# Attention with a routed low-rank layer on one core: how the first head pair and the last weight halves are prepared

## The reference

```
xn = layernorm(x)
q, k, v = xn @ Wq + bq, xn @ Wk + bk, xn @ Wv + bv      # 16 heads of 64
att = softmax(causal(q k^T / 8)) / 8
z = att v, laid out as (s, h * dh) without a transpose of h and s; out1 = z @ proj
base = xn @ W^T
p = l2norm(xn @ Wp^T + bp);  s = l2norm(sim) * exp(min(temp, CLAMP_MAX))
lw = softmax(p @ s);  ret = lw where it is the largest, else 0     # 4 experts
res = sum over the experts of ret * (xn @ Wd_i^T) @ Wu_i^T         # ranks 1, 2, 4, 8
return x + out1 + base + res
```

## Time and profile before

| | us |
|---|---|
| median of 3 runs | 1351.15 |
| lowest and highest of them | 1350.88 and 1351.46 |
| the profiled execution | 1350.67 |
| its span in the trace | 1348.9 |
| of the span: TensorE busy | 1330.2 (99%) |
| VectorE busy | 1106.4 (82%) |
| ScalarE busy | 1086.5 (81%) |
| GpSimd busy | 998.3 (74%) |

### The profile page before, as it was taken

How to read it: one execution, slowest core, us unless ns; L and a number is a source line. 1 busy time by engine, 2 the same in 40 slices (tenths; PEclk the granted TensorE clock), 3 DMA queues, 4 the chain that set the end, 5 groups by cost and what they waited for, 6 DMA issues and landing times.

```text
span 1348.9 us, 34446 instructions
## 1 busy us (share of the span) xinstructions
PE 1330.2 (99%) x10783; PEld 1131.2 (84%) x10783; DVE 1106.4 (82%) x4000; ACT 1086.5 (81%) x3161; POOL 998.3 (74%) x1441
## 2 busy tenths in 40 slices
PE   6999999999999999999999999999999999999998
PEld 4788888888888888888888888888888888888887
DVE  7988888788887878878788787888878888787884
ACT  5887888888878887887888788788888887888785
POOL 6887876778777786777777768777677876778764
PEclk9999999999999999999999999999999999999999
DMA  5444444544545445444544544454454454445441
GB/s 154 103 107 117 114 111 105 128 107 103 124 108 123 98 115 126 103 117 108 120 104 115 124 101 114 113 121 110 104 119 116 103 122 115 118 99 120 112 103 48
DMA packets 112706, 150.85 MB, mean 112 GB/s; under 512 B 18256, under 2 KB 47247, under 8 KB 112527
## 3 DMA queue, kind: packets, MB, share of 16 engines
q1 hardware_dynamic: 111662, 148.36, 46.4%
q10 hardware_dynamic: 864, 0.29, 0.1%
HBM read 10.69 MB, written 4.19 MB: 11 GB/s over the span
## 4 chain that ended last, share of the span: by engine, by line
PE 95%; ACT 1%; DVE 0%; issue 0%
PE zp L1311 22%; PE ptp L1287 20%; PE jobp L1157 13%; PE scores L1275 9%; PE scores L1278 7%; PE outp L1323 7%; PE jobp L1162 6%; PE scores L1256 4%; PE scores L1253 3%; PE jobp L1172 1%; PE outp L1332 1%; ACT prob L720 1%; PE jobp L1177 1%; PE jobp L1348 0%; PE jobp L1167 0%; PE outp L1337 0%
## 5 line engine op out<-in xcount | busy, mean ns | idle before, releaser
L631 POOL TENSOR_TENSOR prob<-prob,rden 128x128 f32<-128x128 f32 (+3 forms) x1024 | 713.9, 722 | 250.7 <-DVE rden L960 244.8
L971 DVE CUSTOM_DVE_ANT_0 prob<-scores,mask 128x128 f32<-128x128 f32 (+3 forms) x1024 | 471.3, 487 | 201.5 <-issue 131.9
L720 ACT ACTIVATE prob<-prob,nmax 128x128 f32<-128x128 f32 (+3 forms) x1024 | 567.5, 559 | 14.7 <-DVE nmax L971 7.8
L1287 PE MATMUL ptp<-ident,prob 128*128 128x128 f32 x2560 | 367.1, 274 | 1.9 <-ACT pt L731 1.5
L1287 PEld LDWEIGHTS ptp<-ident,prob 128*128 128x128 f32 x2560 | 295.0, 140 | 27.7 <-POOL prob L631 4.1
L1311 PE MATMUL zp<-pt,v_sb 128*64 128x64 f32 (+3 forms) x4096 | 307.7, 303 | 0.8 <-DVE z_lo L989 0.8
L731 ACT ACTIVATE pt<-ptp 128x128 f32<-128x128 f32 (+3 forms) x512 | 221.4, 432 | 102.8 <-PE ptp L1287 102.8
L1311 PEld LDWEIGHTS zp<-pt,v_sb 128*64 128x64 f32 x4096 | 221.6, 137 | 51.9 <-issue 20.3
L983 DVE COPY pt<-ptp 128x128 f32<-128x128 f32 (+3 forms) x512 | 243.0, 475 | 3.8 <-PE ptp L1287 2.9
L574 POOL CAST k_low<-k_lo 64x512 fp32r<-64x512 f32 x256 | 156.3, 611 | 77.0 <-DVE k_lo L860 67.0
L1275 PE MATMUL scores<-k_twice,q_parts 128*128 128x384 f32 (+1 forms) x512 | 201.3, 393 | 0.8 <-DVE nmax L971 0.8
(11 more groups left out here) (188 smaller groups left out, 2002.2 us busy)
## 6 DMA issues: line engine op xcount, KB each, us to landing
k_twice<-k_hi SPq DMA_DIRECT2D x508, 128.0 KB, 2.3
q_parts<-q_lo SPq DMA_DIRECT2D x256, 128.0 KB, 2.5
q_parts<-q_hi SPq DMA_DIRECT2D x254, 128.0 KB, 2.3
xin<-in_L_attn_x_dram SPq DMA_DIRECT2D x16, 256.0 KB, 4.2
xres<-in_L_attn_x_dram SPq DMA_DIRECT2D x16, 256.0 KB, 3.1
out_dram<-osb SPq DMA_DIRECT2D x15, 256.0 KB, 2.6
pt<-in_L_attn_Wq_dram SPq DMA_DIRECT2D x1, 512.0 KB, 5.2
pt<-in_L_attn_Wk_dram SPq DMA_DIRECT2D x1, 512.0 KB, 6.1
```

What stands on the lines that cost most here:

```text
L631: nc.gpsimd.tensor_tensor(part, part, scale, ALU.mult).then_inc(pn_ready, 1)
L720: nc.scalar.activation(part, part, ACT.Exp, bias=nmax[:, s % NROT, h:h + 1], scale=-1.0, accum_out=den[:, s % NROT, h:h + 1]).then_inc(p_r ...
L971: nc.vector.tensor_tensor_reduce(out=prob[:, s % NROT, h, 0:cols], in0=scores[bank][:, first_col:first_col + cols], in1=mask[:, S - cols:S ...
L1287: done = nc.tensor.transpose(ptp[h][:, P * j:P * j + P], prob[:, s % NROT, h, P * j:P * j + P], ident[:])
```

## The change

- **Crossing halves.** VectorE makes `swap`, the identity with its column halves exchanged. TensorE multiplies the q low part and `k_hi` of pair 0 by it into `scores[0]` and `outp`. ScalarE copies the results into the other halves of `q_parts` and `k_twice` (four copies of 64 rows by 512). The two DMAs on SP and the two on ScalarE's queue go, and the loads of `proj` no longer wait for them. For pair 1 of the first batch GpSimd copies the two k high parts that stay in their half, and SP issues two DMAs where it issued four. The load of the next batch's `xin` follows the k moves of step 0 and no longer precedes them.
- **The gate's setup.** `sim` and `temp` are loaded by ScalarE's queue at the very start. VectorE's square, sum and clamp, GpSimd's root and ScalarE's exponential move into the gaps of the prologue. `similar_units` runs before the first maximum.
- **The later low halves.** For parts 3, 4, 5 ScalarE makes a second copy of the bank, unrounded, into unused columns of `v_sb` (`raw_weights`). GpSimd subtracts it (`low_weights`, a 128x512 subtraction) at steps 8, 9 and 10, in the order 5, 3, 4. TensorE's jobs of steps 10, 11 and 12 wait for the first, second and third of them. ScalarE does all of parts 3 and 4 after the exponentials of step 0, and evacuates q and k of pair 1 before these.
- **Places in the first batch.** `projection_parts` moves from steps 6 and 10 to 11 and 14, the sum from 14 to 17, `experts_up` from 13 to 18, and the statistics from 5 and 9 to 9 and 17.

```diff
+STEP_SPLIT, STEP_SUMMED, STEP_UP, STEP_BIAS_BANK, STEP_BIAS = (11, 14), 17, 18, 20, 22
+STEP_REST = {8: 5, 9: 3, 10: 4}
+FIRST_STATS = (9, 17)
...
+        w_raw = {k: v_sb[:, k - 2, S:2 * S] for k in (3, 4, 5)}
+        swap = wut
...
+            def low_weights(k):
+                n, half, _ = parts[k]
+                cols = slice(S * half, S * half + S)
+                pool.wait_ge(w_raw_ready, k - 2)
+                nc.gpsimd.tensor_tensor(w_lo[n][:, cols], w_raw[k], w_hi[n][:, cols].bitcast(F32), ALU.subtract)\
+                    .then_inc(w_rest_ready, 1)
...
                     if s in JOBS and JOBS[s][0] == "k" and not (last and s in AHEAD):
                         pad_low_keys(c, s)
+                    if b == 0 and s in STEP_REST:
+                        low_weights(STEP_REST[s])
...
+            def raw_weights(k):
+                nc.scalar.activation(w_raw[k], parts[k][2][:], ACT.Copy).then_inc(w_raw_ready, 1)
...
             job(setup, FIRST_K)
-            act.wait_ge(job_hi[bank_of(FIRST_K)], setup.hi(FIRST_K))
+            act.wait_ge(q_swapped, 1)
             for h in range(2):
-                act.dma_start(k_twice[other(h), h, 0, :].bitcast(F32),
-                              k_hi[own(h), :].bitcast(F32)).then_inc(qk_moved[0], 16)
+                nc.scalar.activation(q_parts[other(h), h, 0, :], scores[0][other(h), :], ACT.Copy).then_inc(crossed, 1)
             weights(2)
-            weights(3)
-            weights(4)
+            act.wait_ge(k_swapped, 1)
+            for h in range(2):
+                nc.scalar.activation(k_twice[other(h), h, 0, :], outp[other(h), :], ACT.Copy).then_inc(crossed, 1)
...
+            pe.wait_ge(swap_ready, 2)
+            pe.wait_ge(job_done[bank_of(FIRST_Q)], setup.job(FIRST_Q))
+            nc.tensor.matmul(scores[0][:], swap[:], q_lo[:, 0, :], start=True, stop=True).then_inc(q_swapped, 1)
+            pe.wait_ge(job_hi[bank_of(FIRST_K)], setup.hi(FIRST_K))
+            nc.tensor.matmul(outp[:], swap[:], k_hi[:], start=True, stop=True).then_inc(k_swapped, 1)
...
+                if first and s in (NBLK * 2 + 2, NBLK * 2 + 3, NBLK * 3):
+                    pe.wait_ge(w_rest_ready, s - NBLK * 2 - 1)
                 if not tail and s in JOBS and not (last and s in AHEAD):
                     job(c, s)
```

More of the change, by code:

```diff
@@ L432, in rows, with move @@
                 return t[bass.ds(b, 1), :, :].rearrange("o (n p) e -> p (o n) e", p=P)
-            def move(c, s):
+            def move(c, s, halves=(own, other)):
                 kind, n = JOBS[s]
@@ L444, in move @@
                     else:
-                        for half in (own(h), other(h)):
-                            sp.dma_start(k_twice[half, h, n % 2, :].bitcast(F32),
+                        for half in halves:
+                            sp.dma_start(k_twice[half(h), h, n % 2, :].bitcast(F32),
                                          k_hi[own(h), :].bitcast(F32)).then_inc(moved, 16)
@@ L457, in batch @@
                 first, last = b == 0 if isinstance(b, int) else False, b is last_batch
-                if not last:
-                    sp.wait_ge(xn_ready, c.at(1, 1))
-                    sp.dma_start(xin[:], rows(x, b + 1)).then_inc(xin_loaded, 16)
                 for s in MOVED_STEPS:
                     if s < STEP_FINAL:
-                        move(c, s)
+                        move(c, s, (other,) if first and s == 0 else (own, other))
+                    if s == 0 and not last:
+                        sp.wait_ge(xn_ready, c.at(1, 1))
+                        sp.dma_start(xin[:], rows(x, b + 1)).then_inc(xin_loaded, 16)
                 if not first:
@@ L480, in _ @@
             sp.wait_ge(job_done[bank_of(FIRST_Q)], setup.job(FIRST_Q))
-            for h in range(2):
-                sp.dma_start(q_parts[other(h), h, 0, :].bitcast(F32),
-                             q_lo[own(h), 0, :].bitcast(F32)).then_inc(qk_moved[0], 16)
-            sp.wait_ge(qk_moved[0], setup.moved(NPAIR))
             for half in range(2):
@@ L599, in _ @@
             pool.wait_ge(heads_marked, 4)
+            pool.wait_ge(job_hi[bank_of(0)], Counts(pool, 0).hi(0))
+            for h in range(2):
+                nc.gpsimd.tensor_copy(k_twice[own(h), h, 1, :], k_hi[own(h), :].bitcast(F32)).then_inc(own_copied, 1)
+            pool.wait_ge(own_copied, 6)
             def projection_parts(half):
@@ L734, in _ @@
             setup = Counts(act, -1)
+            act.dma_start(sim_b[:].rearrange("p a b -> p (a b)"),
+                          sim.rearrange("a b -> (a b)").partition_broadcast(P)).then_inc(sim_loaded, 16)
+            act.dma_start(temp_b[:], temp.partition_broadcast(P)).then_inc(sim_loaded, 16)
             act.wait_ge(zeroed, 3)
@@ L769, in step @@
                 if not tail:
-                    if s - 1 in evacuated(s) and s - 1 in JOBS and not (last and s - 1 in AHEAD):
+                    if s - 1 in evacuated(s) and s - 1 in JOBS and not (last and s - 1 in AHEAD) and not (first and s == 1):
                         job(c, s - 1)
@@ L773, in step @@
                         job(c, UNITS - 1, back=1)
+                    if s == 0 and first:
+                        job(setup, LATER[2])
+                        job(c, 0)
                     if s == STEP_EXPERTS:
@@ L791, in batch @@
                     if first and s == 0:
-                        job(setup, LATER[2])
-                        gate_factor()
+                        for k in (3, 4):
+                            weights(k)
+                            raw_weights(k)
                     if first and s == 1:
                         weights(5)
+                        raw_weights(5)
             batch(0, True, False)
@@ L885, in _ @@
             variances(before)
+            dve.wait_ge(consts_ready, 1)
+            for half in range(2):
+                nc.vector.tensor_copy(swap[:, own(half)], ident[:, other(half)]).then_inc(swap_ready, 1)
             dve.wait_ge(rstd_ready, 1)
@@ L946, in similar_units @@
                 nc.vector.tensor_scalar(simn[:], sim_unit[:], gate_scale[:, 0:1], None, ALU.mult).then_inc(simn_ready, 1)
+            similar_units()
             def value_bias():
@@ L1091, in step @@
                         job(c, js)
-                if s in STEPS_STATS and not last:
-                    statistics(c, STEPS_STATS.index(s))
+                for half, due_step in enumerate(FIRST_STATS if first else STEPS_STATS):
+                    if s == due_step and not last:
+                        statistics(c, half)
                 if s == STEP_AGGR and not last:
@@ L1103, in batch @@
                     if first and s == 0:
-                        weights(3)
                         job(before, LATER[2])
-                    if first and s == 1:
-                        weights(4)
-                        weights(5)
-                    if first and s == 2:
-                        similar_units()
                     if first and s == STEP_UP:
@@ L1262, in score @@
                 if i == 0:
+                    if first and p < 2:
+                        pe.wait_ge(own_copied, 4 + 2 * p)
                     if first and p == 0:
-                        pe.wait_ge(own_copied, 4)
-                    pe.wait_ge(qk_moved[p % 2], c.moved(p))
+                        pe.wait_ge(crossed, 4)
+                    wait(pe, qk_moved[p % 2], c.moved(p))
                     pe.wait_ge(low_padded, c.values(p, 1))
@@ L1295, in values @@
                     wait(pe, z_ready, c.pair(p - 1))
+                    if c.b == 0 and p == 0:
+                        pe.wait_ge(w_raw_ready, 3)
                 if h == 0 and p in (0, NPAIR // 2):
```

50 lines of the change are left out of this document (25 added, 25 removed).

## The result

The changed kernel takes 1356.43 us in the median of six runs (1355.5 to 1357.83), the kernel before 1351.21 beside it. The ratio is 1.0039, with an interval of 1.003 to 1.0049: **5.2 us slower**, and above the range of the forecast (1350.8 to 1356.0). The profiled execution took 1357.83 us (span 1356.1), 7.16 more than the one of before. It is the longest of the six, and one of the two whose mean granted clock was 0.999 and not 1.0. So the two traces differ by 2 us more than the medians, and a reading that sets one trace against the other has to say which part is of the change.

A forecast was written before the change was run, and what follows sets the result against it. TensorE was taken to bound the kernel from about 48 us, so the first batch decides. Terms +0.2 - 0.9 + 4.05 - 0.5 = +2.85 us on a median of 1351.15 gave 1354.0 us, range 1350.8 to 1356.0.

The forecast's parts named there:

- The place: The case is decided in the first batch, before TensorE becomes the bound at about 48 us.
- the chain behind E: GpSimd's pad(3), n(9), n(10) and three subtractions hold TensorE's jobs of steps 10 to 12: +4.05 us.
- E: The end of VectorE's k low part of pair 3 in the first batch, 43.17 us in the kernel before.
- the first loads: Prologue: sim and temp loaded ahead of Wq's end on a second queue cost +0.2 us, ends 0 and +0.4.
- the sum: Whole kernel: +0.2 - 0.9 + 4.05 - 0.5 = +2.85 us on the median.
- The crossing: Prologue: v jobs 0.5 us later, cancelled by ScalarE's earlier q of pair 1; otherwise up to 0.5 lost or 0.3 gained.
- ScalarE at steps 0 to 3: From 19.03 to 28.87 us, 3.2 us of added work into 2.7 of slack makes q of pair 2 +0.3 later.
- E 0.9 earlier: First batch: VectorE's k low part of pair 3 ends 0.9 us earlier, through moved statistics and a shorter router's group.
- The router group: VectorE at step 9, first batch: 1.98 us before, 0.7 us shorter because GpSimd idles then.
- the chain is late as well: Rival, chance 0.20: late k moves of pair 2, dearer first loads and an unshortened router's group give +4.15 us, 1355.3.
- Recovery: After TensorE's job of step 12, two of its waits for ScalarE and VectorE vanish: -0.5 us, ends 0 and 0.9.
- The milepost: Start of TensorE's job of step 12 (k of pair 4), 47.10 us before, forecast near 50; the rest follows at fixed distance.

The follow-up runs named there:

- e2_gate_back: Changed kernel with the gate's loads and setup put back where the kernel before has them: 1355.02 us against 1351.44, ratio 1.0029.
- e5_early_temp: Kernel before with only temp (0.5 KB) loaded by ScalarE's queue at the start, sim staying on SP: 1352.91 us against 1351.51, ratio 1.0011.
- e13_temp_behind: Kernel before with temp on ScalarE's queue but behind ScalarE's first wait, about 0.6 us later: 1351.4 us against 1351.34, ratio 1.0.
- e7_crossing_alone: Changed kernel with the gate's loads and setup put back and the later low halves by VectorE: 1352.66 us against 1351.51, ratio 1.0005.
- e4_lows_dve: Changed kernel with the three later low halves by VectorE after step 1, no raw copies on ScalarE: 1353.64 us against 1351.44, ratio 1.0015.
- e8_hold2: Kernel before with two spare 64 KB loads on SyncE ahead of the k moves of pair 2: 1351.95 us against 1351.51, ratio 1.0005.
- e15_gate_back_rest_early: Changed kernel with the gate put back and GpSimd's three low halves at steps 5, 6, 7: 1353.61 us against 1351.34, ratio 1.0014.

## Why the prediction was wrong

The place was right, and so was the chain behind E; the first loads were priced wrong, and smaller terms erred in the same direction. Without the clock, 5.1 us are to be explained (the four executions at a clock of 1.0 have a median of 1356.3), and the sum said 2.85. By its own terms:

- **First loads, +0.2 with ends at 0 and 0.4: this step failed.** They cost 1.4 us by the changed kernel against e2_gate_back, and 1.4 to 1.75 in the kernel before. The prediction priced 64 KB by a rate, and looked at the end of Wq, the wait that TensorE shows. The transfer that counts is `x`, whose statistics began at 4.04 without a wait to be seen in the earlier trace rows, and moved to 5.88. As far as e5_early_temp and e13_temp_behind go, the price is that of a second queue becoming active as early as the first: they differ in 0.6 us of issue time for 0.5 KB, and in 1.5 us of the kernel's time.
- **The crossing, hidden: right.** In e7_crossing_alone the v jobs are 0.36 later (said: 0.5) and ScalarE's q of pair 1 is 0.22 earlier (said: the shifts cancel, with up to 0.3 to gain). TensorE went on to the v jobs without waiting for the copies. ScalarE's timeline of the changed kernel:

```profile
15.31 1.21 ACT L775 ACTIVATE q_parts<-scores 64x512 fp32r<-64x512 f32 x2 [0.31 <-PE scores L1250]
...
17.23 1.21 ACT L779 ACTIVATE k_twice<-outp 64x512 fp32r<-64x512 f32 x2
```

- **ScalarE at steps 0 to 3, +0.3: a little too high.** ScalarE is without a gap from 20.71 to 34.0 us, as said in kind. From its q of pair 1 to its q of pair 2 it takes 9.14 us in the changed kernel (20.71 to 29.85) and 9.25 in e2_gate_back, against 9.17 in the earlier trace rows.
- **E 0.9 earlier: the path was wrong in part, the size less so.** The prediction took 0.4 off behind q of pair 2, for the statistics moved from step 5, and then 0.15. This saves VectorE time, but the k moves of pair 2 wait for ScalarE: in e2_gate_back q of pair 2 is 0.83 late and the scores of step 8 are 0.83 late. The router group is -0.86, a little more than the 0.7 claimed. In the changed kernel E is 2.75 later; less the 1.84 of `x`, taken as passed on whole, and the 1.58 of the clock that is 0.67 earlier. In e2_gate_back E is where it was, in an execution with the slower prologue. So E by itself lies between -0.67 and 0, and no run here sets it apart from the prologue. The rival "the chain is late as well" had the path of the k moves right, and the router's group wrong. Its reading that these moves gate the scores at 36.91 isn't what the earlier trace rows says either, which names VectorE's maximum; in the changed kernel it is the moves.
- **The chain behind E, +4.05: right.** 4.29 in the changed kernel, 4.30 in e2_gate_back. The third subtraction was said to be ready at E + 7.98, and TensorE's job started at E + 8.22. The waits are another matter: before the job of step 10 TensorE waited 1.27 us and not 2 to 3, because it came to it 1.5 us after E and not 0.4.
- **Recovery, -0.5: failed, not seen in the profiled executions.** The milepost is 7.04 late and the end 7.16 (4.30 and 4.44 in e2_gate_back).
- **The clock: not foreseen.** It cost 1.58 us in the profiled execution. Between the executions of the changed kernel whose mean clock is 0.999, two of six, and the others lie 1.2 us, so it moves the median little. A mean of 0.999 doesn't prove a fall at step 8: the profiled execution of e7_crossing_alone has it too, and no fall there.

The traces add up to the medians. Of the 7.16 us, 1.58 are the clock and 0.54 the quick execution of before, which leaves 5.0, against 5.1 measured at a clock of 1.0. Apart from the clock, the terms in the traces are 1.84 for `x`, -0.67 for the rest of E (a remainder), 4.29 for the chain and 0.12 behind the milepost. The medians divide the loss in their own way: 1.4 for the gate (changed kernel against e2_gate_back), 2.4 for the low halves on GpSimd (e2_gate_back against e7_crossing_alone), 1.15 for the rest (e7_crossing_alone). The last is within the uncertainty of a single run, and e4_lows_dve gives the low halves 2.8. That is less than the 4.29 of the chain, and one reason stands in the traces: with the same work on VectorE, TensorE waits 1.4 us for the maximum at step 3. What no run isolates is the path of ScalarE's three raw copies: they go with the low halves in every pair of kernels compared here.

The rule on the shared port pair, cited in the prediction from the Trainium skill (SBUF — State Buffer, section "SBUF: two separate sides"), agrees with the traces on both sides. L1043's successor fell to 0.17 us with GpSimd idle. L1044, the operation in its place at step 10, took 1.17 us from 47.53, while GpSimd's first low half ran from 47.41 to 48.67. In the prologue `sim_unit` took 1.26 us from 18.30 (0.61 before), beside a GpSimd addition from 18.11 to 19.40. The stretches were moved, not removed.

## What to carry to other kernels

Ask of a load that is moved to the front what else is on its way then, and follow the first transfer that an engine needs, also where the engine that bounds the kernel shows its wait for another one; 0.5 KB on a second queue can cost as much as 64 KB, and a delay of 0.6 us can make it free. Where work is handed to an engine that stands in a chain, sum from the event that starts the chain, and move both ends: an earlier place shortens what comes behind the event and delays the event itself. A profiled execution that is longer than the median may hold an effect that most executions don't have; the granted clock by 1 us stretches can find it, and where that reads 1.00, the length of like products in two traces. And a trace of before that is quicker than its median makes every comparison with it too large.

## What the runs showed of the hardware

- A load of 0.5 KB to 128 partitions, issued on ScalarE's queue at the same 0.79 us as `x` (256 KB) on SyncE's, made `x` land 4.2 us after issue and not 3.2; issued 0.6 us later it left `x` at 3.1. With sim's 64 KB at the head, alone or with temp, it was 4.9. Why the head start matters this much is not settled. The Trainium skill (DMA: Bandwidth & Descriptors, section "Queues, rings and completion order") says that each DMA engine takes turns between the queues it has work for, a packet at a time. By that alone temp would cost `x` as much 0.6 us later, which these runs don't show.
- TensorE's granted clock fell to 0.50 behind stands of 2.06, 2.15 and 2.62 us, for 3 to 7 us, and did not behind stands of 2.03, 1.67 and 1.52. These are single executions, and how busy TensorE had been before each stand was not varied.
- The first 128x512 product of the program takes 0.71 to 0.78 us in every trace that can be read, and how long such products stay slow differs: until about 10.2 us in before and e7_crossing_alone, until 12.8 in e8_hold2 and e13_temp_behind, until 14.5 in e2_gate_back. The granted clock reads 1.00 in all of them, so the lengths show it and the column does not.
- SyncE's four k moves of pair 2 took 2.4 to 2.5 us to issue in eight of the traces (2.52 in e15_gate_back_rest_early) and 3.5 to 4.2 in the other nine that can be read (3.85 in before, 4.16 in the changed kernel). These moves gate step 8 in most of the runs, and what stretches their issue stays open.
